# Offset convolution by pairs of batches and float32 scores for batch 0 in a four-layer kernel

## The reference

```python
# layer 2: 32x32 queries, each over a 7x7 window of keys, 4 batches, 4 heads
attn = jnp.einsum('bnijd,bnipjqd->bnijpq', q, k_win) + bias[None]
attn = jax.nn.softmax(attn.reshape(B_, nh, H_, W_, k * k), axis=-1)
...
# layer 4: a 3x3 convolution gives two offsets per channel and pixel, x is sampled there
offsets = lax.conv_general_dilated(x, W, window_strides=(1, 1), padding='SAME', ...) + b   # W: [3, 3, 32, 64]
...
c0 = jnp.clip(coords[..., 0], 0.0, jnp.float32(w - 1))
c1 = jnp.clip(coords[..., 1], 0.0, jnp.float32(h - 1))
...
mapped = vals_t + (vals_b - vals_t) * f1
```

## Time and profile before

| | |
|---|---|
| Median of 3 runs | 800.01 us (797.45 to 803.14) |
| The profiled execution's own time | 799.63 us |
| Its span, first to last instruction | 797.8 us |
| Busy: PE, DVE, ACT, POOL | 81%, 85%, 67%, 57% |
| Mean granted TensorE clock | 0.91 |
| Attention's scores to last values | about 134.7 to 238.4 us |
| Scan | about 311.7 to 630 us |
| Offset convolution | 641.1 to 672.2 us |
| Sampling loop with its start | 674.6 to 790.9 us |

### The profile page before, as it was taken

How to read it: one execution, slowest core, us unless ns; L and a number is a source line. 1 busy time by engine, 2 the same in 40 slices (tenths; PEclk the granted TensorE clock), 3 DMA queues, 4 the chain that set the end, 5 groups by cost and what they waited for, 6 DMA issues and landing times.

```text
span 797.8 us, 12457 instructions
## 1 busy us (share of the span) xinstructions
PE 648.7 (81%) x4051; PEld 406.6 (51%) x4051; DVE 677.0 (85%) x955; ACT 531.3 (67%) x657; POOL 455.2 (57%) x285
## 2 busy tenths in 40 slices
PE   7899998579998962676677777767767898999996
PEld 5555546468884310254444454544545643556563
DVE  7899988559975789999899999998999724899996
ACT  2666514559984568677776877777767301999994
POOL 3788863100002066899899999898998601422221
PEclk9999999789999995689987898998988999999999
DMA  2014101551002032000000000000000002100001
GB/s 54 5 16 103 17 2 30 76 105 33 4 3 83 3 87 43 1 0 1 1 1 1 0 1 1 0 1 0 1 1 0 1 1 52 27 0 0 0 0 27
DMA packets 30034, 15.62 MB, mean 20 GB/s; under 512 B 23982, under 2 KB 25902, under 8 KB 29838
## 3 DMA queue, kind: packets, MB, share of 16 engines
q1 hardware_dynamic: 29694, 14.56, 8.8%
q0 software_dynamic: 288, 0.39, 0.3%
HBM read 5.76 MB, written 0.78 MB: 8 GB/s over the span
## 4 chain that ended last, share of the span: by engine, by line
PE 42%; DVE 35%; issue 7%; POOL 5%; ACT 5%; SPq 4%; DVEq 0%; DMA 0%; POOLq 0%; ACTq 0%
PE ps L550 35%; DVE arena L1339 12%; DVE ps L1012 8%; DVE arena L1012 4%; DVE arena L1058 4%; SPq L378 4%; PE ps L975 4%; POOL arena L1728 3%; PE ps L732 3%; DVE ps L1058 2%; POOL x3t L1728 1%; ACT arena L1687 1%; POOL xn L1728 1%; DVE arena L1282 1%; ACT x L1687 1%
## 5 line engine op out<-in xcount | busy, mean ns | idle before, releaser
L550 PE MATMUL ps<-arena 128*64 128x64 f32 (+4 forms) x1992 | 344.4, 342 | 111.1 <-DVE arena L1339 37.7
L550 PEld LDWEIGHTS ps<-arena 128*64 128x64 f32 (+4 forms) x1992 | 141.8, 142 | 227.8 <-issue 81.5
L1728 POOL TENSOR_TENSOR arena<-arena 128x1024 f32<-128x1024 f32 x81 | 188.2, 2335 | 24.1 <-DVE arena L1339 8.6
L1339 DVE TENSOR_TENSOR_SCAN arena<-arena,ps 128x1024 f32<-128x1024 f32 x66 | 150.9, 2287 | 8.6
L1012 DVE TENSOR_TENSOR ps<-arena,ps 128x1024 f32<-128x1024 f32 x75 | 90.9, 1212 | 7.7 <-PE ps L550 6.9
L1713 ACT ACTIVATE arena<-ps,nycol 128x1024 f32<-128x1024 f32 x64 | 70.5, 1101 | 36.2 <-PE ps L550 36.2
L1674 ACT ACTIVATE arena<-arena,a_col 128x1024 f32<-128x1024 f32 x66 | 75.4, 1142 | 17.1 <-DVE arena L1339 16.8
L1847 POOL TENSOR_TENSOR arena<-arena,bmask 128x128 f32<-128x128 f32 x64 | 30.2, 472 | 84.6 <-PE ps L550 76.0
L1571 ACT ACTIVATE arena<-arena 128x256 f32<-128x256 f32 x128 | 60.8, 503 | 22.3 <-DVE arena L1220 17.8
L1339 DVE TENSOR_TENSOR_SCAN arena<-ps,arena 128x1024 f32<-128x1024 f32 x30 | 68.2, 2272 | 2.7 <-POOL arena L1728 2.6
L550 PE MATMUL ps<-ident,arena 128*128 128x128 f32 x416 | 63.7, 305 | 2.0 <-POOL arena L1728 2.0
(11 more groups left out here) (196 smaller groups left out, 1155.9 us busy)
## 6 DMA issues: line engine op xcount, KB each, us to landing
arena<-arena SPq DMA_DIRECT2D x66, 64.0 KB
arena<-arena SPq DMA_DIRECT2D x12, 128.0 KB, 3.3
w_conv<-in_c_far SPq DMA_DIRECT2D x1, 1152.0 KB, 5.7
w_conv<-rpb_pad SPq DMA_DIRECT2D x36, 28.0 KB, 1.8
arena<-x SPq DMA_DIRECT2D x12, 64.0 KB, 2.0
arena<-x1t SPq DMA_DIRECT2D x12, 64.0 KB, 2.0
arena<-x3t SPq DMA_DIRECT2D x12, 64.0 KB, 2.0
x<-in_x SPq DMA_DIRECT2D x1, 512.0 KB, 3.3
```

The lines of the kernel that those rows point to most:

```text
L550: return pe.matmul(o, l, r, start=start, stop=stop, **k)
L1339: ve.tensor_tensor_scan(hs_ring[n % RING], decay, add, 0.0, ALU.mult, ALU.add).then_inc(S("scan"), 1)
L1728: return gp.tensor_tensor(o, a, b, ALU.mult)
```

## The change

Three parts. (1) In the attention all 8 groups of batch 0 multiply float32 tiles: `k_own` gets two more tiles (in `xn` and `x3t`), which ACT makes from PSUM ahead of the exponentials. Batch 0's 18 row DMAs and `qk_rows` go; SP starts with batch 1, and PE waits on each batch's DMA semaphore. (2) The offset convolution computes batches 0 and 1 (p = 0) and 2 and 3 (p = 1) apart, each with both offset components as 128 output rows. Each pair of batches has an image of 128 rows: its own 64 rows, and in the other 64 the same rows moved by one pixel, copied by a DMA. So one product of 128 rows does taps kx = 0 and 1. Tap kx = 2 is done from the 64 own rows alone, partitions 0 to 63 for p = 0 and 64 to 127 for p = 1, in turn. `xrow` becomes two tiles, each filled up by a DMA on ACT's queue. (3) The transposes of `x3t` come before the convolution, ACT copies them to `x3_row`; after the loop POOL subtracts for batches 0 and 1, DVE for 2 and 3, and the output is stored by batch from SP and ACT.

```diff
-        q_own, k_own = x1, [x0, grid_x]
+        q_own, k_own = x1, [x0, grid_x, xn, x3t]
...
-            for b in range(B):
-                if b >= 2:
-                    eng.wait_ge(s_ld[f"qk{b % 2}"], QK_LOADS - (0 if b % 2 else QK_POOL))
-                    if b == 3:
-                        eng.sem_inc(S("qk_rows"), 1)
+            for b in range(1, B):
+                if b == 3:
+                    eng.wait_ge(s_ld["qk1"], QK_LOADS)
...
-            for b in range(2, B):
-                eng.wait_ge(s_ld[f"qk{b % 2}"], QK_LOADS * 2 - (0 if b % 2 else QK_POOL))
-                eng.sem_inc(S("qk_rows"), 1)
...
+            eng.wait_ge(S("gn"), 3)
+            eng.dma_start(flat_image[0][DI:P, 0:WP * WP - 1], flat_image[0][0:DI, 1:WP * WP]).then_inc(s_ld["image"], 16)
+            eng.wait_ge(S("gn"), 4)
+            eng.wait_ge(s_ld["image"], 16)
+            eng.dma_start(flat_image[1][0:DI, 1:WP * WP], flat_image[1][DI:P, 0:WP * WP - 1]).then_inc(s_ld["image"], 16)
...
+            eng.wait_ge(S("yout_first"), 2)
+            for b in range(2):
+                store(eng, b, slice(0, NBLK))
             for h in range(2):
                 eng.wait_ge(S("yout"), h + 1)
-                for k in range(4 * h, 4 * h + 4):
-                    eng.dma_start(out.rearrange("b h w c -> (h w) b c")[P * k:P * k + P], yout[:, k]).then_inc(S("stored"), 16)
-            eng.wait_ge(S("stored"), 16 * NBLK)
+                store(eng, 2, slice(4 * h, 4 * h + 4))
+            eng.wait_ge(S("stored"), 16 * 6)
...
-                        if g < OWN // GROUP:
-                            last = mm(o, q_own[:, queries], k_own[h][:, keys])
+                        if b == 0:
+                            last = mm(o, q_own[:, queries], k_own[2 * m + h][:, keys])
...
-                if g == OWN // GROUP:
-                    pe.wait_ge(s_ld["qk0"], QK_LOADS - QK_POOL)
-                    pe.wait_ge(s_ld["qk_pool"], QK_POOL)
+                if g == GPB // 2:
+                    pe.wait_ge(S("k_heads"), 2)
                 if g and g < NGROUP and g % GPB == 0:
-                    pe.wait_ge(S("qk_rows"), above(g // GPB))
+                    b = g // GPB
+                    pe.wait_ge(s_ld[f"qk{b % 2}"], QK_LOADS * (2 if b == 3 else 1))
...
-            keep_busy(6, 13)
-            pe.wait_ge(s_ld["conv"], 16 * B)
-            pe.wait_ge(S("gn"), 3)
-            for par_ in range(2):
-                for k in range(9):
-                    ky, kx = divmod(k, 3)
+            keep_busy(6, 5)
+            pe.wait_ge(S("x3t"), 2)
+            for c in range(NBLK):
+                last = pe.transpose(ps[:, 2 + c // 4, P * (c % 4):P * (c % 4) + P], x3t[:, P * c:P * c + P], ident[:])
+            last.then_inc(S("x3_turned"), 1)
+            keep_busy(6, 4)
+            pe.wait_ge(s_ld["conv"], 16 * 8)
+            for ky in range(3):
+                for h in range(2):
+                    for p in range(PAIRS):
+                        if ky == 0 and h == 0:
+                            pe.wait_ge(S("gn"), 3 + p)
+                        mm(ps[:, 6 * p + h, :], w_taps[DI * p:DI * p + DI, 1, ky], native(p, ky + 16 * h, 2),
+                           start=(ky == 0), stop=False)
+            for p in range(PAIRS):
+                bank = 6 * p
+                pe.wait_ge(s_ld["image"], 16 * (p + 1))
+                for ky in range(3):
                     for h in range(2):
-                        last = mm(ps[:, 2 * par_ + h, :], w_conv[:, k, par_],
-                                  xpad[:, ky + 16 * h:ky + 16 * h + 16, kx:kx + C], start=(k == 0), stop=(k == 8))
+                        last = mm(ps[:, bank + h, :], w_taps[:, 0, ky], image[p][:, ky + 16 * h:ky + 16 * h + 16, 0:C],
+                                  start=False, stop=(ky == 2))
                 last.then_inc(S("conv"), 1)
             pe.wait_ge(s_ld["rows0"], 16 * 6)
             pe.wait_ge(s_ld["b4"], B4_LOADS)
-            pe.wait_ge(S("coord"), 2)
+            pe.wait_ge(S("coord"), 1)
+            pe.wait_ge(S("x3_row"), 1)
...
+                        if first and t == LAG_POS:
+                            pe.wait_ge(S("coord"), 2)
...
-            pe.wait_ge(S("abs"), above(NJ * NT))
-            for c in range(NBLK):
-                last = pe.transpose(ps[:, c // 4, P * (c % 4):P * (c % 4) + P], x3t[:, P * c:P * c + P], ident[:])
-            last.then_inc(S("x3_turned"), 1)
...
+                if into is None:
+                    for p in range(PAIRS):
+                        r = slice(DI * p, DI * p + DI)
+                        ve.tensor_scalar(image[p][r, 1:1 + C, 1 - p:1 - p + C], x[r].rearrange("p (h w) -> p h w", w=C),
+                                         small[r, 20:21], small[r, 24:25], ALU.subtract, ALU.mult).then_inc(S("gn"), 1)
+                    return
...
-            ve.transpose(xrow, inside.rearrange("p r c -> p c r")).then_inc(S("xrow"), 1)
+            for p in range(PAIRS):
+                r = slice(DI * p, DI * p + DI)
+                ve.wait_ge(S("gn"), 3 + p)
+                ve.transpose(xrow[p][r], image[p][r, 1:1 + C, 1 - p:1 - p + C].rearrange("p r c -> p c r")).then_inc(S("xrow"), 1)
...
             for h in range(2):
-                tt(yout[:, 4 * h:4 * h + 4].rearrange("p k b (g j) -> p k (b g) j", g=CGRP),
...
+                finish(ve, 1, h).then_inc(S("yout"), 1)
...
+            ac.activation(k_own[3][:], bank2(2), ACT.Identity, bias=sees_bias[:, 3:4], scale=sees[:, 3:4]).then_inc(S("k_heads"), 1)
+            ac.wait_ge(S("v"), 5)
+            ac.activation(k_own[2][:], bank2(2), ACT.Identity, bias=sees_bias[:, 2:3], scale=sees[:, 2:3]).then_inc(S("k_heads"), 1)
...
+            ac.wait_ge(S("x3_turned"), 1)
+            ac.activation(x3_row, bank2(2), ACT.Copy).then_inc(S("x3_row"), 1)
+            ac.wait_ge(S("xrow"), 1)
+            ac.dma_start(xrow[0][DI:P], xrow[0][0:DI]).then_inc(s_ld["xrow"], 16)
+            ac.wait_ge(S("xrow"), 2)
+            ac.wait_ge(s_ld["xrow"], 16)
+            ac.dma_start(xrow[1][0:DI], xrow[1][DI:P]).then_inc(s_ld["xrow"], 16)
...
+            gp.wait_ge(S("x3_row"), 1)
+            gp.wait_ge(S("summed"), above(CPER * NT))
+            for h in range(2):
+                finish(gp, 0, h).then_inc(S("yout_first"), 1)
```

More of the change, by code:

```diff
@@ L302, in build @@
         cv.at = scan_at
-        xpad = cv(WP, WP)
-        xrow = cv(C, C)
+        image = [cv(WP, WP) for _ in range(2)]
+        xrow = [cv(C, C) for _ in range(2)]
+        x3_row = cv(T)
         coord = cv(2, T)
@@ new lines, in _ @@
+            for r in range(4):
+                shift, b = divmod(r, 2)
+                taps = d["wconv"].rearrange("c (y x) o n -> c x y o n", x=3)
+                for k in range(2):
+                    to = w_taps[C * r:C * r + C, k].rearrange("p y (o b n) -> p y o b n", o=2, b=2)[:, :, :, b]
+                    eng.dma_start(to, taps[:, (shift, 2)[k]]).then_inc(s_ld["conv"], 16)
+            eng.wait_ge(S("gn"), 3)
+            eng.dma_start(flat_image[0][DI:P, 0:WP * WP - 1], flat_image[0][0:DI, 1:WP * WP]).then_inc(s_ld["image"], 16)
```

132 lines of the change are left out of this document (70 added, 62 removed).

## The result

The changed kernel takes 779.98 us (median of 4 runs, 776.66 to 782.24) where the kernel before takes 799.82 (4 runs, 797.45 to 803.14): a ratio of 0.9747, 95% interval 0.9716 to 0.9779. The gain is 19.8 us of the 24.7 forecast; the time lies in the range, 4.8 us above the predicted 775.2. The profiled execution took 779.18 us, with a span of 777.4.

The account below looks back on a forecast made before the run. PE was taken to set the pace in attention, convolution and loop. Gains of 8.7 (attention), 12.3 (convolution to loop start) and 3.7 (end) sum to 24.7 us: 799.63 becomes 774.9, stated as 775.2; range 770 to 782.

Parts of the forecast that it names:

- Attention, 8.7 us: Attention: float32 scores make a pass 3.83 us but remove PE's breaks; gain 8.7 us, bounds 6.5 to 9.5.
- rival (c): Attention: breaks are not removed, PE still waits for batch 1's rows, part gives 0; 783.9 us, chance 0.03.
- ACT's two extra key tiles at nothing: Attention start: two more key tiles, 1.20 us each, delay the exponentials but cost nothing; without PE's idle cover 1.0 us.
- Single taps side by side, 5.2 us for twelve: Offset convolution: 64-row products on different rows run fully side by side, 5.2 us; one after the other 10.3.
- Rival (a): Offset convolution: single taps don't run side by side, everything behind comes 5.2 us later; 780.4 us, chance 0.13.
- Convolution 15.9 us: Offset convolution: about 15.9 us from its first to its last record.
- Image copies hidden: Offset convolution: DMA copies of the image, taken as 4 us, are hidden behind products; 0.8 us at the bad end.
- PE's wait before the loop, 5.3 us: Between convolution and loop: PE stands idle 5.3 us until the coordinate DMAs land.
- Rival (b): Loop start: the longer idle time costs more clock, four more slow steps, 4 us; 779.2 us, chance 0.10.
- Rival (d): Loop: the low clock does not recover, each step costs 1.0 us more; 815 us at 40 steps, chance 0.02.
- The end, 3.7 us: Kernel end: split subtraction and earlier stores gain 3.7 us, bounds 2 to 4.2.
- The scan and the loop keep their instructions: Scan and the loop's steady state: instructions stay the same, so no gain or loss was put in the sum.

Follow-up runs that it names:

- layer4_only: The changed kernel with the attention of the kernel before; layer 4 and the stores stay changed: 786.37 us, ratio 0.9822.
- attention_only: The kernel before with only the attention part of the change: 791.8 us against 799.5, ratio 0.9915.
- four_groups: The changed kernel with float32 scores only in groups 0 to 3 of batch 0, bf16 again in groups 4 to 7: 782.24 us against 798.59, ratio 0.9788.
- both_and_split: The changed kernel with idle-time products at the scan's end and before the loop, and three of six coordinate DMAs on ACT's queue: 773.88 us, ratio 0.9677.
- busy_before_loop: The changed kernel with 24 idle-time products in PE's wait for the first coordinate rows before the loop: 775.64 us, ratio 0.9719.

## Why the prediction came out as it did

**Attention, 8.7 us: right.** Pass of 3.83 us, no break between 140 and the last values, batch 1's rows in time. From before's profile to the changed one the stretch gave 10.0 us, of which 1.4 is the projection's clock by the luck of the execution, so the term measured 8.6. Against the smaller second break of layer4_only it is 6.9, and 6.8 by attention_only's runs: a term read from one profile of a break that varies carries that profile's luck. The rival (c), that breaks stay, is out; four_groups shows how near it lay, with a break of 4.85 us for four fewer float32 groups.

**ACT's two extra key tiles at nothing: right.** PE waited 1.54 us ahead of its first transposes, 1.55 before.

**Single taps side by side, 5.2 us for twelve: right.** Two loads per 0.43 us. Rival (a) would have added 5.2; even six and six in turn cost only 2.75.

**Convolution 15.9 us: measured 16.7.** Half of the excess is the first pair's product, which has no partner until the second normalization, 0.8 us for which I charged 0.4. Some 0.2 us is at the change from 64 to 128 rows: the weight load comes after 0.76 us of idle loads instead of 0.24, and the matmul records there start 0.52 and 0.53 us apart instead of 0.43. The semaphore wait on the image that stands there is not the reason: the same wait ahead of the second pair's 128-row products costs nothing (0.43 us). The Trainium skill ("TensorEngine Tiling (Array Packing)", key properties) says that a change of tiling mode drains the array. The row of the load at 640.23, which comes so late, agrees. The last 0.2 us is the very last record: the sum took it at 0.43 us, and its own length is 0.59.

**Image copies hidden: right**, 3.9 us against the 4 that I took.

**PE's wait before the loop, 5.3 us: measured 6.2, the mis-sized term.** DVE's last coordinate instruction ended at 650.69 + 1.23 = 651.92, PE started at 656.97: 5.05 us, where I had summed 4.0, for one issue ahead (0.59) and a landing of 3.3, the median. The trace has the landing itself: the sixth DMA was issued at 652.57 and landed 4.35 us later, at 656.92. In the kernel before it was 4.34 us, hidden behind PE's other products, and its largest landing stood in the row that I took the median from, 4.3. The landing is long because five others are on their way: the six land at 651.88, 653.03, 654.13, 655.13, 656.19 and 656.92, 0.7 to 1.2 us apart, and both_and_split shows that issuing the last ones earlier doesn't bring them in earlier. Convolution, wait and start together: 10.9 us instead of 12.3.

**Rival (b), a longer idle time costs clock: did not happen.** The clock was 0.59 over the first 8 us after 0.54 before, and the way to the first sum 8.23 us after 8.35. The forecast of "the same" was right for a reason that I hadn't given: ACT's pace bounds the first steps, as busy_before_loop shows. The rival's price was badly founded too: 14 records in 7.4 us are, at eight a step, 4.2 us a step and not 2.7. The trace of the kernel before has the spreads of its third to fifth step at 2.17, 4.77 and 7.64 us after the first product, so 2.6 to 2.9 apart, which is near 2.7 but isn't how I got it. Rival (d) is out with it: the loop was at a full clock from 665 on.

**The end, 3.7 us: measured 3.0.** The order of events was right. The last store, ACT's second, is issued 1.1 us after the last sum where I took 0.9, and lands after 2.4 us in place of 1.9. It has the size of the old ones, 64 KB, but another queue and another layout; which of these costs the 0.5 us, the runs don't separate.

**"The scan and the loop keep their instructions": the step that failed.** They do, and the loop kept its time within 0.4 us. But I took it that the rest keeps its time too. The scan took 1.2 us more in this profile and the way to the convolution 2.4, together most of the 4.3 us that are missing. The first lies within what the same code shows from one execution to the next (309.8 to 312.3 us), and its cause stays open. The second goes with the low clock behind PE's two waits for POOL, whose cause the runs don't show; in the two further profiles of the change it was +2.3 and +0.7. The kernel before, with 12.56 in its profile, had lost 0.6 there itself. In the sum: 24.7 forecast, less 1.4 for convolution and wait, 0.7 for the end, 1.2 scan, 2.4 clock and 0.4 loop, plus 1.4 for the projection's clock and 0.6 in the head, is 20.6 for a measured 20.4.

## What to carry to other kernels

Products with few rows are worth placing on different rows and issuing in turn: each pair then costs one product, for the price of one copy of the data to the other half and here about 0.2 us at the change to full rows. When a wait ends with several DMAs in flight, use the slowest landing in the sum, not the median, and don't expect a second queue to shorten it. Before a low clock is charged to an edit, ask whether PE is what the stretch waits for, and whether the same code loses it in every execution. A part that an edit doesn't touch still needs bounds of its own, from two profiles if possible: here it moved by 3 to 4 us, on a forecast of 24.7.

## What the runs showed of the chip that was not expected

- PE began weight loads and matmuls for the other row group about four records ahead of their turn: 12 single taps in two blocks of six cost 2.75 us more than in alternation, not 5.2.
- Two 128 KB DMAs issued at the same time on two queues landed 0.9 to 1.1 us apart, three times in a row, and the last of six took 5.13 us in place of the 4.35 it took when issued 0.6 us later.
- PE stopped for 3.09 and 3.15 us in the middle of a group's transposes, after the same sixth one in two profiles, with nothing to wait for in the profile, after 498 and 474 records without a new packet on the instruction queue q8; in five other kernels these were at most 354 to 391, and there was no such gap. Row DMAs held about half of the DMA engines.
- PE waits of 1.2 to 2.0 us were followed by a low granted clock (0.50 at the scan's end) in some executions and by a full clock in others, at three places of the program, worth 1.4 to 3.0 us each. Three kernels with filler at one of them didn't lose it there, which three cases don't prove to be the filler's doing.
- A low clock at the loop's start cost 0.8 us where its records took 1.8 times as long.
